# Relative attention on one core: softmax denominators from ScalarE's accumulator, numerators summed in their final rows, key copies on VectorE

## What is computed

```
q = x @ Wq + bq;  k = ctx @ Wk + bk;  v = ctx @ Wv + bv          # 16 heads of 16
attn = softmax((q k^T + q . rel_k[clip(j - i)]) / 4)              # 100 x 361 for each head
out = (attn @ v + sum_j attn[i, j] rel_v[clip(j - i)]) @ Wo + bo
x = layernorm(x + out)
```

## Time and profile before

| | |
|---|---|
| median of 3 runs | 2637.18 us (2627.58 to 2637.78) |
| profiled execution, its own time | 2634.07 us |
| its span | 2632.4 us |
| busy: PE, DVE, ACT, POOL | 88%, 57%, 48%, 24% |
| the stage of the change | about 1397 to 2232 us of the span |

### The profile page before, as it was taken

The page is one execution under the profiler, slowest core; times in us unless marked ns, Lnnn a source line. Parts: engine busy times, 40 slices in busy tenths (PEclk is TensorE's granted clock), DMA queues, the critical chain, the costliest instruction groups (busy, mean ns, idle before and its releaser), DMA issues. The chain is left out here.

```text
span 2632.4 us, 51884 instructions
## 1 busy us (share of the span) xinstructions
PE 2306.5 (88%) x17888; PEld 1841.9 (70%) x17888; DVE 1491.6 (57%) x2871; ACT 1260.4 (48%) x2706; POOL 631.2 (24%) x690
## 2 busy tenths in 40 slices
PE   8989999957999999929996999999999997894057
PEld 5769999946999999928884777777677675552045
DVE  5766666646111113228884666666666664545865
ACT  2223333331434444417774666666666664436743
POOL 1101111137344444444452112111211210000000
PEclk9999999967999999969998999999999997897579
DMA  2132222155899999840014555555555551010111
GB/s 84 39 91 69 68 68 68 46 172 177 284 344 343 342 344 345 278 135 2 0 19 103 127 140 128 129 139 129 129 140 129 130 135 43 38 57 0 69 36 38
DMA packets 375996, 339.28 MB, mean 129 GB/s; under 512 B 70226, under 2 KB 351852, under 8 KB 374636
## 3 DMA queue, kind: packets, MB, share of 16 engines
q1 hardware_dynamic: 311148, 294.61, 37.7%
q10 hardware_dynamic: 52480, 26.83, 4.0%
q0 software_dynamic: 12288, 16.79, 2.9%
HBM read 254.83 MB, written 83.37 MB: 128 GB/s over the span
## 5 line engine op out<-in xcount | busy, mean ns | idle before, releaser
L2298 ACT COPY rel_probT<-rel_ps_t 121x400 f32<-121x400 f32 x384 | 193.5, 504 | 174.6 <-PE rel_ps_t L2513 174.6
L2310 ACT ACTIVATE rel_prob<-rel_ps_s,rel_nmx 100x361 f32<-100x361 f32 x512 | 263.6, 576 | 2.0 <-DVE rel_nmx L2386 1.9
L2513 PE MATMUL rel_ps_t<-rel_ident,rel_prob 100*121 100x100 f32 x1536 | 240.3, 279 | 6.7 <-ACT rel_probT L2298 6.7
L2513 PEld LDWEIGHTS rel_ps_t<-rel_ident,rel_prob 100*121 100x121 f32 x1536 | 203.6, 187 | 58.6 <-issue 20.8
L1392 PEld LDWEIGHTS moe_ps_h<-moe_xeT,moe_w 128*128 128x128 f32 x2048 | 240.0, 193 | 5.1 <-issue 1.9
L1392 PE MATMUL moe_ps_h<-moe_xeT,moe_w 128*128 128x128 f32 x2048 | 240.6, 276 | 1.3 <-DVE moe_xeT L1552 1.3
L2386 DVE TENSOR_REDUCE rel_nmx<-rel_ps_s 100x2 f32<-100x722 f32 x256 | 232.8, 909 | 8.8
L1392 PE MATMUL moe_ps_y<-moe_w,moe_hT 128*128 128x256 f32 x1024 | 231.4, 379 | 0.0
L3027 PE MATMUL ffd_ps_y<-ffn_w_dT,ffd_oq 128*100 128x256 f32 x384 | 86.4, 387 | 139.8 <-DVE ffd_oq L2972 134.2
L1383 ACT ACTIVATE moe_hT<-moe_ps_h,moe_b 128x128 f32<-128x128 f32 x512 | 142.8, 376 | 137.1 <-PE moe_ps_h L1392 136.8
L1392 PEld LDWEIGHTS moe_ps_y<-moe_w,moe_hT 128*128 128x128 f32 x1024 | 189.6, 190 | 23.2
(11 more groups left out here) (430 smaller groups left out, 4908.4 us busy)
## 6 DMA issues: line engine op xcount, KB each, us to landing
moe_w<-in_L_ffn_w SPq DMA_DIRECT2D x128, 1024.0 KB
rel_scores<-rel_r_ext SPq DMA_DIRECT2D x32, 818.8 KB
rel_r_key<-rel_scores SPq DMA_DIRECT2D x32, 818.8 KB
rel_weights<-rel_prob ACTq DMA_DIRECT2D x128, 204.7 KB
rel_by_dist<-rel_weights SPq DMA_DIRECT2D x32, 393.8 KB
mut_ctx_nat<-in_ctx SPq DMA_DIRECT2D x32, 363.0 KB
mut_ctx_T<-in_ctxT SPq DMA_DIRECT2D x16, 722.0 KB
rel_ctx_T<-in_ctxT SPq DMA_DIRECT2D x32, 361.0 KB, 9.4
```

Of the source, the lines that this page charges most:

```text
L2298: nc.scalar.copy(probT[:, pg % 2, c], ps_pT).then_inc(s_t_sb, 1)
L2310: last = nc.scalar.activation(prob[:, t.parity, slot, :], ps_s[0:S, j, 0:L], ACT.Exp, bias=nmx[:, slot:slot + 1])
L2513: last = nc.tensor.transpose(ps_pT[:, j, :], prob[:, pt.parity, QUAD * pg + j, c * STEP:c * STEP + R], ident[0:S, 0:S])
```

## The change

Three things are changed. (1) The exponentials get an accumulator output: ScalarE adds up each row of weights while it takes the exponentials, so the tile `den` holds the 16 denominators of a row. VectorE inverts them (100 x 16) at the start of the next turn and spreads each over 16 columns (`den_wide`, 100 x 256); job `den` becomes two products of `den_wide` with the identity that transpose it (128 x 100 each), and VectorE only copies the result. (2) The half of `vals` beside each head's values is zero and the two groups of a row block are summed into the same rows of PSUM, so `raw` (now 128 x 200) stands in the final layout; job `w2` loses its two products by `pick`, and VectorE adds `raw` and multiplies by `rec` in two instructions. (3) The copies of the keys with their bias (`k0`, `k1`) go from ScalarE to VectorE, and job `out` moves from place 14 to place 15, behind T2 of the last group. Some constants are no longer made.

```diff
-            nc.gpsimd.memset(self.vals[:], 1.0).then_inc(s_const, 1)
+            nc.gpsimd.memset(self.vals[:], 0.0).then_inc(s_const, 1)
...
@@ -2104,7 +2093,11 @@
         far = m.sb("far", [S, NH, FAR])
         by_dist = m.sb("by_dist", [S, NH, ND])
         distT = m.sb("distT", [P, PAIRS, S])
-        raw = m.sb("raw", [P, GROUPS, S])
+        raw = m.sb("raw", [P, KC, S])
+        den = m.sb("den", [S, 2, NH])
+        den_rec = m.sb("den_rec", [S, NH])
+        den_wide = m.sb("den_wide", [S, NH, HD])
+        mixed = m.sb("mixed", [P, KC, S])
         rec = m.sb("rec", [P, KC, S])
         attT = m.sb("attT", [P, KC, S])
         ps_m = m.ps("ps_m", [P, 2, 512])
...
@@ -2112,7 +2105,7 @@
         ps_t = m.ps("ps_t", [P, 512])
         ps_o = m.ps("ps_o", [P, 512])
         ps_pT = ps_t[0:R, 0:QUAD * S].rearrange("p (j s) -> p j s", j=QUAD)
-        ps_raw = ps_o[:, 0:GROUPS * S].rearrange("p (g s) -> p g s", g=GROUPS)
+        ps_raw = ps_o[:, 0:KC * S].rearrange("p (c s) -> p c s", c=KC)
 
         sem = m.sem
         s_const, s_ctx = ahead.s_const, ahead.s_ctx
...
@@ -2139,7 +2133,7 @@
         JOBS = [("after", "xT"), ("next", "k0"), ("after", "q"), ("next", "k1"), ("after", "r0"), ("next", "v0"),
                 ("last", "den"), ("after", "r1"), ("next", "v1"), ("next", "v2"), ("last", "d0"), ("last", "d1"),
                 ("last", "w2"), ("last", "out")]
-        PLACES = [[0], [1], [2], [3], [4], [5], [6], [7], [], [8], [9], [10], [11], [12], [13], []]
+        PLACES = [[0], [1], [2], [3], [4], [5], [6], [7], [], [8], [9], [10], [11], [12], [], [13]]
         NUMBER = {what: n for n, (_, what) in enumerate(JOBS)}
 
         def bank(what):
...
@@ -2254,7 +2248,7 @@
 
             turns(pool, turn, -2, 3, B - 3, B + 1)
 
-        ON_ACT = ("xT", "r0", "r1", "k0", "k1", "d0", "d1")
+        ON_ACT = ("xT", "r0", "r1", "d0", "d1")
 
         @block.scalar
         def _(act):
...
@@ -2282,10 +2276,6 @@
                     h = int(what[1])
                     nc.scalar.copy(distT[:, h * PAIRS // 2:(h + 1) * PAIRS // 2, :], bank(what)[:, 0:PAIRS // 2 * S].rearrange(
                         "p (n s) -> p n s", n=PAIRS // 2)).then_inc(s_job_sb[n % 2], 1)
-                else:
-                    c = int(what[1])
-                    nc.scalar.activation(kT[:, b.parity, c, :], bank(what)[:, 0:L], ACT.Identity,
-                                         bias=k_bias[:, c:c + 1]).then_inc(s_job_sb[n % 2], 1)
 
             def transposed(pt, pg, c):
                 if not pt.within(B):
...
@@ -2305,10 +2295,12 @@
 
                     act.wait_ge(s_pout[t.parity], 16 * GROUPS * t.half)
                     act.wait_ge(s_far, t.i - 1)
+                    act.wait_ge(s_den, t.i - 1)
                 for j in range(2 * k, 2 * k + 2):
                     slot = QUAD * g + j
                     last = nc.scalar.activation(prob[:, t.parity, slot, :], ps_s[0:S, j, 0:L], ACT.Exp,
-                                                bias=nmx[:, slot:slot + 1])
+                                                bias=nmx[:, slot:slot + 1],
+                                                accum_out=den[:, t.parity, slot:slot + 1])
                 last.then_inc(s_p if k else s_half, 1)
 
             def store(b, g):
...
@@ -2360,11 +2352,18 @@
                     halves = vals[:, b.parity, c].rearrange("p (k e) (x d) -> p k (e x) d", e=2, x=2)[:, :, 0:4:3, :]
                     nc.vector.tensor_tensor(halves, bank(what)[0:R, 0:D].rearrange("p (k e d) -> p k e d", k=PAIRS, e=2),
                                             v_bias[:].rearrange("p (k e) d -> p k e d", e=2), ALU.add).then_inc(s_job_sb[n % 2], 1)
+                elif what in ("k0", "k1"):
+                    c = int(what[1])
+                    nc.vector.tensor_scalar(kT[:, b.parity, c, :], bank(what)[:, 0:L], k_bias[:, c:c + 1], None,
+                                            ALU.add).then_inc(s_job_sb[n % 2], 1)
                 elif what == "den":
-                    nc.vector.reciprocal(rec[:], two(what)).then_inc(s_job_sb[n % 2], 1)
+                    nc.vector.tensor_copy(rec[:], two(what)).then_inc(s_job_sb[n % 2], 1)
                 elif what == "w2":
+                    dve.wait_ge(s_att, b.i + 1)
+                    nc.vector.tensor_tensor(mixed[:], two(what), raw[:], ALU.add).then_inc(s_mix, 1)
+                    dve.wait_ge(s_mix, b.i + 1)
                     wait_emptied(dve, t, "den")
-                    nc.vector.tensor_tensor(attT[:], two(what), rec[:], ALU.mult).then_inc(s_job_sb[n % 2], 1)
+                    nc.vector.tensor_tensor(attT[:], mixed[:], rec[:], ALU.mult).then_inc(s_job_sb[n % 2], 1)
                 elif what == "out":
                     dve.wait_ge(s_xb, b.i + 1)
                     nc.vector.tensor_tensor(at(y_nat, b.i), bank(what)[0:S, 0:D], at(y_nat, b.i), ALU.add).then_inc(s_job_sb[n % 2], 1)
...
@@ -2393,6 +2392,15 @@
                 nc.vector.tensor_scalar(xn[:], at(y_nat, b.i), mean[:, bass.ds(b.i, 1)],
                                         rstd[:, bass.ds(b.i, 1)], ALU.subtract, ALU.mult).then_inc(s_xn, 1)
 
+            def invert(b):
+                dve.wait_ge(s_p, GROUPS * b.i + (GROUPS + 1))
+                nc.vector.reciprocal(den_rec[:].rearrange("p (c j e) -> p c j e", c=KC, e=2),
+                                     den[:, b.parity].rearrange("p (c e j) -> p c j e", c=KC, e=2)).then_inc(s_den, 1)
+                dve.wait_ge(s_den, b.i + 1)
+                if not isinstance(b.i, int) or b.i > 0:
+                    wait_filled(dve, b, "den")
+                nc.vector.tensor_copy(den_wide[:], den_rec[:].unsqueeze(2).to_broadcast([S, NH, HD])).then_inc(s_wide, 1)
+
             def turn(t):
                 prev = t + -1
                 if isinstance(t.i, int) and t.i == -2:
...
@@ -2401,6 +2409,8 @@
                     dve.wait_ge(s_ready, 1)
                 for g in range(GROUPS):
                     maxima(t, g, 0)
+                    if g == 0 and prev.within(B):
+                        invert(prev)
                     if g == 1 and prev.within(B):
                         dve.wait_ge(s_pv, GROUPS * prev.i + GROUPS)
                         nc.vector.tensor_copy(raw[:], ps_raw).then_inc(s_att, 1)
...
@@ -2468,18 +2478,16 @@
                 elif what == "den":
                     if isinstance(b.i, int) and b.i == 0:
                         pe.wait_ge(s_ready, 1)
-                    pe.wait_ge(s_att, b.i + 1)
-                    for e in range(2):
-                        last = mm(two(what), swap[:, e, :], raw[:].rearrange("p (c e) s -> p e c s", e=2)[:, e], e, 2)
+                    pe.wait_ge(s_wide, b.i + 1)
+                    for c in range(KC):
+                        last = mm(two(what)[:, c, :], den_wide[:, c * HC:(c + 1) * HC, :].rearrange("p h d -> p (h d)"),
+                                  ident[0:S, 0:S], 0, 1)
                 elif what == "w2":
-                    for e in range(2):
-                        nc.tensor.matmul(two(what), pick[:, e, :], raw[:].rearrange("p (c e) s -> p e c s", e=2)[:, e],
-                                         start=(e == 0), stop=False)
                     wait_emptied(pe, t, "d1")
                     for q in range(QUAD):
                         last = nc.tensor.matmul(two(what), tab_v_wide[:, q, :],
                                                 distT[:].rearrange("p (c q) s -> p q c s", c=KC)[:, q],
-                                                start=False, stop=(q == QUAD - 1))
+                                                start=(q == 0), stop=(q == QUAD - 1))
                 else:
                     wait_emptied(pe, t, "w2")
                     for k in range(KC):
...
@@ -2525,8 +2533,8 @@
                 for c in range(CH):
                     r = R if c == CH - 1 else STEP
                     for j in range(QUAD):
-                        last = mm(ps_raw[j * TILE:(j + 1) * TILE, pg, :], vals[0:r, pt.parity, c, head_of(pg, j), :],
-                                  probT[0:r, pg % 2, c, j, :], c, CH)
+                        last = mm(ps_raw[j * TILE:(j + 1) * TILE, pg // 2, :], vals[0:r, pt.parity, c, head_of(pg, j), :],
+                                  probT[0:r, pg % 2, c, j, :], CH * (pg % 2) + c, 2 * CH)
                 last.then_inc(s_pv, 1)
 
             def turn(t):
```

More of the change, by code:

```diff
@@ L1645, in __init__ @@
         self.ident = m.sb("ident", [P, P])
-        self.pick = m.sb("pick", [P, 2, P])
-        self.swap = m.sb("swap", [P, 2, P])
         self.ctx_T = m.sb("ctx_T", [P, 2, KC, L])
@@ L1735, in value_tables @@
                 at_ = TILE * (2 * (q % 2) + i) + HD * (q // 2)
-                nc.vector.tensor_copy(self.tab_v_wide[i * ND:(i + 1) * ND, q, at_:at_ + HD], self.tab_v[i * ND:(i + 1) * ND, :])
-        for e in range(2):
-            nc.vector.tensor_scalar(self.pick[:, e, :], self.ident[:], self.parity[:, e:e + 1], None, ALU.mult)
```

(4 more changed lines are left out.)

13 lines of the change are left out of this document (5 added, 8 removed).

## The result

The changed kernel took **2643.61 us** (median of 8 runs, 2639.87 to 2646.92), the kernel before 2632.49 (8 runs, 2627.58 to 2637.78). The ratio is **1.0045**, with an interval of 1.0033 to 1.0058: slower, by 8.7 to 15.3 us. I had written that 0.5% is about what a measurement of this kernel can tell from no change; this one was finer. The forecast was 2645 with a range of 2625 to 2662. The profiled executions have spans of 2643.0 and 2632.4 us. Of the twelve executions of `both_moves` (experiment 7) one took 3492.76 us at a mean granted clock of 0.64; its median and ratio are those of the other eleven.

What follows compares the result with a forecast made beforehand. Two nearly equal chains, TensorE's work and ScalarE's copies and exponentials, bound the kernel; -0.27 + 0.20 + 0.33 + 0.08 = +0.34 us a turn, +10.5 us, less 2 once, gave 2642.6, forecast as a 2645 us median, range 2625 to 2662.

Steps and rivals of the forecast that it cites:

- both chains trade: The forecast case: the change takes from TensorE's work and gives to ScalarE's chain, +8.5 us; chance 0.57.
- The sum a turn: The four parts added for one turn of the middle stage: +0.34 us, or +10.5 us over the turns.
- the one-time term: Last sequence: reciprocal leaves the path and `pick` products go, against an added instruction; 2 us saved, between 0 and 4.
- Part 1: Last group: `pick` products removed and `out` moved; of 0.70 us removed, 0.27 us a turn is won.
- part 4: VectorE's first group: added work and key copies end late, so `k1` waits for its bank, +0.08 us a turn.
- Part 2: Job `den`: products of about 0.4 us instead of 0.70, gaining nothing because TensorE waits for ScalarE there.
- Part 3: Accumulator reads after exponentials: +0.20 us in group 1, +0.33 through group 2 to `d1`, covered in groups 0 and 3.
- rival E: TensorE's new holes in the last group and near `den` lower its clock: 3 us a turn, 2730 us; chance 0.04.
- B: TensorE's work bounds everywhere: 1.0 us a turn saved, 2604 us; chance 0.15 together with the case of wholly hidden reads.
- C: Accumulator reads before a copy do not overlap, 0.20 us each: +0.94 us a turn, 2664 us; chance 0.14.
- D: VectorE's first group ends last and TensorE waits for the emptied bank of `k0`: 2654 us; chance 0.10.

Runs made afterwards that it cites:

- both_moves: Changed kernel with its jobs reordered (`r0` before `v0`, `v1` and `k1` later) and VectorE making the second transposed-weight copies of groups 1 and 2: 2637.67 us, ratio 1.0021.
- experiment 7: Changed kernel with VectorE instead of ScalarE making the second transposed-weight copies of groups 1 and 2: 2627.80 us, ratio 0.9983; also run with reordered jobs as `both_moves`.
- experiment 4: Changed kernel without accumulator reads (denominators constant) and with the key copies back on ScalarE: 2627.57 us, ratio 0.9982 to the kernel before.

## Why the prediction was right

The sign and the mechanism hold: both chains trade, and the reads cost where ScalarE is waited for. The sum a turn was 0.10 us too high and the one-time term too low, and these two errors go in opposite directions.

- **Part 1 (-0.27).** Measured -0.18. The step in group 3 was sound: T1 to the next scores was forecast at 2.59 and is 2.61, group 3 fell by 0.23. What was missing from the term is that a later `out` makes VectorE late in the next group 0 also where the keys stay on ScalarE: that group grows by 0.05 us on the mean (experiment 4); part 4 had counted this delay only in front of the key copy. And the move of `out`, of which I had written that it only opens a hole which C1 and T2 fill, costs 0.12 against leaving it at place 14.
- **Part 2 (0).** Borne out. T2 behind `den` waits for ScalarE with the shorter `den` as before: the new products last 0.61 us instead of the 0.87 by `swap`, and without reads group 1 takes 6.56 us, as in the kernel before.
- **Part 3 (+0.20 and +0.33).** Measured +0.18 and +0.30 (0.16 in group 2 and 0.14 at the split scores), by the kernels with and without reads. From C0 of group 2 to `d1` it is 3.91 us (2013.34 to 2017.25) where it was 3.61. I had placed all of this at the split scores; half of it is already lost in front of T2 of group 2, whose weight load waits for C1, and since both stand in the same ScalarE chain the sum is the same. I had taken 0.10 a read and it is 0.09. That groups 0 and 3 cover their reads was stated, and the run with reads in two groups shows it for the changed kernel: with half the reads the turn is the same.
- **Part 4 (+0.08).** Its mechanism is there in half the turns: `k1` waits 0.12 us for the emptied bank in every second one, and place 14 takes that away. But on balance the key copies on VectorE save 0.06 us a turn without reads (24.65 to 24.59), and 0.26 beside the reads in the kernel before. I had left them as a gain "in places where it does not end last", and with reads it ends last in more places. The Trainium skill's rule on copies within SBUF (VectorE: DVE Perf Modes, The perf-mode tier table) is borne out: `den_wide`, 100 x 256, takes 0.29 us instead of the 0.43 that I had taken.
- **The turn.** -0.18 + 0.48 - 0.06 = +0.24, as measured; the forecast was +0.34.
- **The one-time term (-2) is not there in the trace.** The stage's end is 2.4 us longer in it. Behind the last full turn it is 1.0 us shorter (15.6 us to the last addition to `y`, from 16.6): the reciprocal's wait is gone, but the next thing late was a transfer. What is lost is in the last full turn, which begins at 2196.29 and ends at 2226.64: it takes 30 us instead of the 27.4 of before, with its clock at half for most of the time:

```profile
2190.00:2200.00 10.00, 8.49 (x100) 6.05 (x96) 6.80 (x14) 6.28 (x20) 2.31 (x1) 1.00 0.17 42
2200.00:2210.00 10.00, 8.95 (x60) 6.26 (x60) 4.92 (x8) 5.77 (x18) 0.00 (x0) 0.52 0.31 67
2210.00:2220.00 10.00, 8.84 (x80) 6.05 (x76) 4.34 (x8) 4.66 (x13) 0.00 (x0) 0.50 0.15 38
```
```profile
2198.99 0.67 PE L2521 MATMUL rel_ps_t<-rel_ident,rel_prob 100*121 100x100 f32 x4 [0.58 <-ACT rel_probT L2288]
...
2204.32 1.13 PE L2521 MATMUL rel_ps_t<-rel_ident,rel_prob 100*121 100x100 f32 x4
...
2232.17 1.18 PE L2433 MATMUL rel_ps_m<-rel_ident,rel_den_wide 100*128 100x100 f32 x4
2234.03 1.57 PE L2476 MATMUL rel_ps_m<-rel_ident,rel_by_dist 100*128 100x100 f32 x8 [0.68 <-DMA rel_by_dist<-rel_weights]
```

The granted clock goes from 1.00 to 0.50, 2.4 to 1.2 GHz, behind waits of 0.58 and 0.81 us in front of two transposes 1.5 us apart, and four transposes go from 0.67 to 1.13 us. `d0` of the last sequence (2234.03) waits 0.68 for the transfer `rel_by_dist`, where the earlier trace rows had 1.50 for the reciprocal. This is rival E's mechanism, but I had priced it for the middle of the stage, where the clock stays at 1.00. The page that I had cited for it (the Trainium skill, TensorE: Matmul & The Clock Gate, A second HAM failure mode: psum-queue depth-cycling) speaks of short frequent holes; the holes of the middle, 0.37 and 0.58 us once a turn each, do not bring it about, and the middle is at 1.00 in every kernel here; it is in the stage's first and last turns, which lack some of the jobs, that the clock falls in each. That the holes are the cause there is argued and not tested.
- So the turns, +7.4 us for 31 instead of +10.5, and the rest, about +3 or 4 instead of -2, make a total near the forecast. That the total came out within 1.4 us is luck twice over. The two errors cancel in part. And the forecast was built on the three runs of the kernel before that were known, whose median was 2637.18, while with eight it is 2632.49: as a difference I had forecast +8, and +11.1 was measured.
- **Rivals.** B, TensorE as the bound everywhere (2604), is refuted: with less work on TensorE in every turn the kernel is slower. It was also tested from the other side, since without the reads, when ScalarE is as fast as before, the gain is 0.24 us a turn and not 1.0. C (nothing overlaps behind a read) is refuted by the 0.09 us from a read to the copy behind it (2009.09 to 2009.18, where the read lasts 0.21). D is real, but only 0.06 us a turn, and comes with the place of `out`.

What stays open: why VectorE's first addition of distance scores comes 0.24 us late in every second turn (its row names only "issue"; with `out` at place 14 it is late too and nothing waits for it), and what sets the clock of the last turns, where one profiled execution of each kernel is compared with one of another.

## What to carry to other kernels

Where two engines' chains end within 0.1 or 0.2 us of each other, price a change by place and not by engine: here sixteen reads cost as much as the eight that stand where ScalarE is waited for (and more where it had the key copies as well), and the same move of two copies was worth 0.26 us beside those reads and 0.07 without them. Before adding a small instruction to a chain that is waited for, take something out of it: two copies a turn moved to the less busy engine turned a loss of 0.45% into a gain of 0.17%. And moving a product behind a wait does not fill the hole; look who starts from that product on the next engine.
